# Attention pass of a four-layer graph network: where chunk sums, block steps and turned scores stand in VectorE's, ScalarE's and TensorE's order

## The chip, the cores and the metric

The kernel runs on one core of one Trainium2 chip. The metric is the device time of one execution in microseconds (us). Before the change it was 3532.23 us, the median of three runs (3505.18 to 3546.59).

## What is computed

A graph of 3125 nodes with 256 features and 53125 edges, sorted by their destination, goes through four graph layers, each with a residual and a layer norm. Only the first, an attention layer, is touched here:

```python
Q = (h @ Wq).reshape(n, H, HD); K = ...; V = ...            # 8 heads of 32
score = einsum('ehd,ehd->eh', Q[dst], K[src]) / sqrt(HD)
score = score + relu(efeat @ W1 + b1) @ W2 + b2             # a small MLP on 64 edge features
m = segment_max(score, dst); ex = exp(score - m[dst])
alpha = ex / segment_sum(ex, dst)[dst]
out = segment_sum(alpha * V[src], dst) @ Wo + bo
x = layernorm(x + out)
```

## The kernel before

The edges stand in tiles of 128; eight tiles are a *group* (1024 edges, 52 groups). Key and value rows of a group's sources are gathered into a ring of four buffers by indirect DMAs that GpSimd issues. A *chunk* is the group shifted by one tile; its value sums are added up one group behind the scores. A *block* is 128 destination nodes; every second group finishes one block, four pairs of groups behind.

The attention pass is one function `fused(g, k, i, b)` for each engine, run for group after group by `each_four` (L401): the first twelve groups are written out, then a loop takes four at a time, then two more. There is no planner: each engine runs its instructions in the order of its `fused`, and semaphores hold it back. A group with even k is called *even* here and one with odd k *odd*.

What one group g does, by the names in the code:

- TensorE: `turn_weights` (L1207) turns back the exponentials of chunk g-1. `q_rows` (L1183), once for each half, builds the query rows of four tiles in PSUM banks 0 and 1, which both halves share. `hidden` (L1155) is the MLP's first layer for group g+1. `tile_sums` (L1218) sums weighted value rows of chunk g-1, a half at a time. `turn_scores` (L1195) turns the scores of group g. `mlp_scores` (L1164) and `scores_back` (L1175) end the MLP for g+1. `window_sums` (L1234) puts the chunk's sums into their window of nodes. An even group ends with `turn_rows` (L1269) of a block, an odd one has `turn_back` (L1289) in its middle and `product` (L1296), the block's output projection, at its end.
- VectorE: `half_scores` (L1747), once for each half, multiplies query rows with gathered keys and reduces over a head (L1752, L1756). `weigh` (L1772, operations at L1780) multiplies value rows by their weights. `add_mlp` (L1759) finishes the scores of the group; `make_oht` and `make_narrow` build one-hots; `shift_scores` (L1794) runs two scans and a subtraction on the turned scores. `add_chunk` (L1808) adds the window sums to the accumulator, after a load of the window's first column from `chunk_i` into a register. For a block there are `rows_step` and `bias_step` (L1840, L1884), `norm_stats` (L1899) after the projection, and `norm_apply` (L1917) after ScalarE's two square roots.
- ScalarE: `weights_copy`, four `relu` (L840) on the MLP's hidden layer, `roots` (L912), `finish_rows` (L920), `stage_block` (L881), `turn_block` (L900), `sums_copy` (L862), `mlp_copy` (L842), and `exponent` (L848).

In VectorE's order before, a group ends with `shift_scores(g)`, then `add_chunk(g-1)`, then `rows_step` and `bias_step` (even) or `norm_stats` (odd). `add_chunk` waits for the window sums, `norm_stats` for the product. Then comes `half_scores(g+1, 0)`, which waits for `q_rows(g+1, 0)`.

Of the kernel before, what the change touches and what calls it, by code (L numbers as in the profile page):

```python
# [22 lines left out]
NG = -(-E // EG)  # L23
# [7 lines left out]
LAG = 3  # L31
# [8 lines left out]
CHUNKS = NG + 1  # L40
# [14 lines left out]
PASS_NONE, PASS_VALUE, PASS_GCN1, PASS_GCN2, PASS_SAGE, PASS_SG1, PASS_SG2, PASS_SG3 = range(8)  # L55
# [11 lines left out]
def gnn_program(nc, a, out):  # L67
    ctx = ExitStack()
    with ctx:
# [722 lines left out]
        def _(act):  # L792
# [40 lines left out]
            def windows_path():  # L833
                def relu(g, u):

                    c, half = u // 2, u % 2
                    act.wait_ge(hid_done, g * 4 + (u + 1))

                    wait(act, mlp_done, g)
                    nc.scalar.activation(hid[:, u, :], banks[:, 2 + half, :], ACT.Relu, bias=b1c[:, c:c + 1]).then_inc(hid_evac, 1)  # L840
# [13 lines left out]
                def weights_copy(c, k):  # L854
                    act.wait_ge(ex_back, c + 1)

                    wait(act, val_done, c * 2 - 2)
                    nc.scalar.activation(xcol[:, k, :, HEADS + 1:XW], ew_pad[:, bass.ds(c * TG, TG)].unsqueeze(2), ACT.Copy)
                    nc.scalar.activation(xcol[:, k, :, 0:HEADS], banks[:, S_BANK, EX_AT:EX_END].rearrange("p (t h) -> p t h", h=HEADS), ACT.Copy
                                         ).then_inc(ex_copied, 1)  # L860
# [39 lines left out]
                def turn_block(q, b):  # L900
                    if q in DENSE:
                        bank_sem = pe_a if q == PASS_SAGE else pe_b
                        before = blocks_before(q) + 1 if q == PASS_SAGE else blocks_before(q, TURNED)
                        act.wait_ge(bank_sem, b + (before + 1))
                        nc.scalar.activation(turned[:, :, :], banks[:, B_TURN, 0:D].rearrange("p (c n) -> p c n", c=FC), ACT.Copy  # L905
                                             ).then_inc(turn_done, 1)
# [53 lines left out]
                def fused(g, k, i, b):  # L960
                    full = not isinstance(g, int) or g < NG
                    blocks = not isinstance(b, int) or b >= 0
                    c, kc = g - 1, (k + 1) % 2
                    if not isinstance(g, int) or g:
                        weights_copy(c, kc)
                    if not isinstance(b, int) or b > 0:
                        if k % 2 == 0:
                            roots(PASS_VALUE, b - 1)
                    if full:
                        relu(g + 1, 0)  # L970
                        relu(g + 1, 1)
                    if blocks and k % 2 == 1:
                        turn_block(PASS_VALUE, b)
                    if not isinstance(b, int) or b > 0:
                        if k % 2 == 0:
                            finish_rows(PASS_VALUE, b - 1)
                    if full:
                        relu(g + 1, 2)
                        relu(g + 1, 3)
                    if blocks and k % 2 == 0:  # L980
                        stage_block(PASS_VALUE, b)
                    if not isinstance(g, int) or g:
                        sums_copy(c)
                    if full:
                        mlp_copy(g + 1, kc)
                    if not isinstance(g, int) or g < CHUNKS:
                        exponent(g)
# [81 lines left out]
        def _(pe):  # L1069
# [84 lines left out]
            def windows_path():  # L1154
# [28 lines left out]
                def q_rows(g, half):  # L1183

                    if half == 0:
                        pe.wait_ge(oht_ready, g + 1)
                    pe.wait_ge(qwin_done[half], g * 32 + 32)
                    wait(pe, qk_read, g * 2 + half)
                    for m in range(2):
                        for r in range(2):  # L1190
                            last = nc.tensor.matmul(banks[:, r, m * D:(m + 1) * D], oht[r * QW:(r + 1) * QW, half, m * P:(m + 1) * P],  # L1191
                                                    q_win[r * QW:(r + 1) * QW, half, :], start=True, stop=True)
                    last.then_inc(q_done, 1)
# [130 lines left out]
                def fused(g, k, i, b):  # L1324
                    full = not isinstance(g, int) or g < NG
                    value = not isinstance(g, int) or g > 0
                    blocks = not isinstance(b, int) or b >= 0
                    kc, kn = (k - 1) % RING, (k + 1) % 2
                    loads = (g + 1) // 2 + 1 if isinstance(g, int) else i * 2 + ((k + 1) // 2 + 1)
                    if value:  # L1330
                        turn_weights(g - 1)
                    if full:
                        q_rows(g, 0)
                        hidden(g + 1, kn, loads, 0)
                        q_rows(g, 1)
                    if blocks and k % 2 == 1:
                        wait(pe, chunk_added, g - 1)
                        turn_back(PASS_VALUE, b)
                    if full:
                        hidden(g + 1, kn, loads, 1)  # L1340
                    if value:
                        if blocks and k % 2 == 1:
                            pe.wait_ge(rows_done, b + 1)
                            pe.wait_ge(turn_done, b + 1)
                        elif blocks:
                            wait(pe, var_done, b)
                        tile_sums(g - 1, kc, 0)
                        tile_sums(g - 1, kc, 1)
                    if not isinstance(g, int) or g < CHUNKS:
                        turn_scores(g, k, i)  # L1350
                    if full:
                        mlp_scores(g + 1)
                        scores_back(g + 1, kn)
                    if value:
                        window_sums(g - 1, kc)
                    if blocks and k % 2 == 0:
                        turn_rows(PASS_VALUE, b)
                    if blocks and k % 2 == 1:
                        product(PASS_VALUE, b)
# [76 lines left out]
        def _(dve):  # L1436
# [24 lines left out]
            chain = Chain(link_sem)  # L1461
# [263 lines left out]
            def windows_path():  # L1725
# [237 lines left out]
                chain_at, size = chain_total(chain), LINKS[PASS_VALUE]  # L1963

                def fused(g, k, i, b):
                    static = isinstance(g, int)
                    full, value = not static or g < NG, not static or g > 0
                    blocks = not isinstance(b, int) or b >= 0
                    c, kc = g - 1, (k - 1) % RING
                    before = not static or b > 0  # L1970
                    if blocks and k % 2 == 0:
                        chain.enter(b * size + (chain_at - 4) if before else chain_at)
                    if full:
                        half_scores(g, k, i, 0)
                    if before and k % 2 == 0:
                        norm_apply(PASS_VALUE, b - 1)
                    if value:
                        weigh(c, kc, 0)
                    if full:
                        half_scores(g, k, i, 1)  # L1980
                    if value:
                        weigh(c, kc, 1)
                    if full:
                        add_mlp(g, k)
                        if k == RING - 1:
                            wrap_scores(i)
                        make_oht(g + 1)
                    if not static or g < CHUNKS:
                        make_narrow(g, k % 2)
                        shift_scores(g, k % 2, (g // 2 + 1) * (16 * TG) if static else i * (RING // 2 * 16 * TG) + (k // 2 + 1) * (16 * TG))  # L1990
                    if value:
                        add_chunk(c)
                    if blocks and k % 2 == 0:
                        rows_step(PASS_VALUE, b)
                        bias_step(PASS_VALUE, b)
                    if blocks and k % 2 == 1:
                        norm_stats(PASS_VALUE, b)
                        assert chain.leave() == (size if before else size - 4)

                each_four(dve, fused)  # L2000
                chain.enter(chain_at + (NG // 2 - LAG) * size - 4)
                norm_apply(PASS_VALUE, NG // 2 - LAG - 1)
                for b in range(NG // 2 - LAG, NB):
                    rows_step(PASS_VALUE, b)
# [3 lines left out]
                for q in GROUPED:  # L2008
# [44 lines left out]
                    size = LINKS[q]  # L2053
# [115 lines left out]
```

## Time and profile before

| | before |
|---|---|
| median of 3 runs | 3532.23 us |
| profiled execution | 3527.64 us |
| its span | 3525.7 us |
| TensorE busy | 2560.2 us (73%) |
| VectorE busy | 1970.7 us (56%) |
| GpSimd busy | 1737.9 us (49%) |
| ScalarE busy | 682.7 us (19%) |

The span is the time from the first to the last instruction of the profiled execution. The attention pass lies between about 126 us, where VectorE's first score product starts, and 1060 us; three gather passes and three dense passes follow. Busy shares are averages over all of these, so they say little of the attention pass: its own windows and its own chain of waits have to be read.

### The profile page before, as it was taken

How to read it: one execution, taken by the hardware profiler on the slowest of the kernel's cores; microseconds unless marked ns; L12 is line 12 of the kernel's file. 1: busy time of each engine (PE TensorE's matmuls, PEld its weight loads, DVE VectorE, ACT ScalarE, POOL GpSimd, SP SyncE). 2: the span in 40 equal slices, each digit the busy share in tenths (PEclk: the TensorE clock that was granted, in tenths of full speed). 3: DMA queues.
4: the chain of work that ended last, by engine and by line, in shares of the span. 5: the costliest groups of instructions: out<-in, count | busy, mean ns of one | idle time of the engine just before them, and what ended most of it. 6: DMA issues, size and time to landing. Idle time of an engine off the chain costs nothing.

```text
span 3525.7 us, 64349 instructions
## 1 busy us (share of the span) xinstructions
PE 2560.2 (73%) x18318; PEld 1985.6 (56%) x18422; DVE 1970.7 (56%) x6179; ACT 682.7 (19%) x1571; POOL 1737.9 (49%) x1779
## 2 busy tenths in 40 slices
PE   7566767666765565556767676577777699999997
PEld 6344334434435555554555555456665478888775
DVE  3477777676756555556667676667767621111222
ACT  3223333333330000001111111011111231111110
POOL 0554444444407777776777776677777500000000
PEclk9788887787766878787889888798889889999998
DMA  5876555565503333333333343333333322332221
GB/s 187 246 208 175 173 173 170 164 179 166 170 20 101 109 110 111 109 110 95 114 120 115 117 123 97 91 116 115 118 112 113 97 79 98 103 102 93 88 96 58
DMA packets 185480, 435.80 MB, mean 124 GB/s; under 512 B 42835, under 2 KB 89161, under 8 KB 185417
## 3 DMA queue, kind: packets, MB, share of 16 engines
q0 software_dynamic: 93184, 272.74, 26.7%
q1 hardware_dynamic: 88634, 159.04, 13.9%
q10 hardware_dynamic: 3600, 3.28, 0.3%
q8 instruction: 29, 0.48, 0.1%
q14 instruction: 33, 0.27, 0.0%
HBM read 390.37 MB, written 44.51 MB: 123 GB/s over the span
## 4 chain that ended last, share of the span: by engine, by line
PE 31%; POOL 26%; issue 21%; DVE 13%; DMA 6%; ACT 2%; SPq 1%; DVEq 1%; POOLq 0%; ACTq 0%
POOL gath L767 25%; PE banks L1411 15%; DVE prod L1752 3%; PE banks L1256 3%; DMA gath<-h_table,idx_slot 3%; PE banks L1239 2%; PE banks L1170 2%; DVE rh L1756 2%; DVE gath L1780 2%; DVE rh L1780 2%; PE banks L1303 1%; PE banks L1227 1%; DMA misc<-counts 1%; PE banks L1080 1%; PE banks L1242 1%
## 5 line engine op out<-in xcount | busy, mean ns | idle before, releaser
L767 POOL DMA_INDIRECT gath<-h_table,idx_slot x1248 | 1293.2, 1036 | 371.3 <-issue 344.5
L1256 PE MATMUL banks<-onehot,gath 128*128 128x128 f32 x4992 | 782.6, 323 | 479.8 <-DMA gath<-h_table,idx_slot 451.6
L1256 PEld LDWEIGHTS banks<-onehot,gath 128*128 128x128 f32 x4992 | 730.8, 233 | 538.0 <-DMA gath<-h_table,idx_slot 452.2
L1411 PE MATMUL banks<-gath,misc 128*128 128x256 bf16 x1875 | 516.5, 275 | 0.0
L1411 PE MATMUL banks<-acc,misc 128*128 128x256 bf16 x2500 | 421.4, 277 | 23.4 <-DMA misc<-counts 14.5
L765 POOL DMA_INDIRECT rh<-kv_table,idx_slot x208 | 211.1, 1015 | 215.3 <-PE banks L1230 163.1
L765 POOL DMA_INDIRECT gath<-kv_table,idx_slot x208 | 209.0, 1005 | 214.0 <-PE banks L1230 159.7
L1314 PE MATMUL banks<-gath 128*128 128x512 bf16 x624 | 243.7, 414 | 64.7 <-DVE gath L1958 64.7
L1411 PEld LDWEIGHTS banks<-acc,misc 128*128 128x128 bf16 x2500 | 243.4, 99 | 70.3 <-issue 16.8
L1958 DVE TENSOR_SCALAR gath<-w_qkv 128x800 bf16<-128x800 f16 x728 | 257.5, 424 | 0.0
L1838 DVE TENSOR_TENSOR acc<-acc,banks 128x256 f32 x156 | 65.3, 418 | 339.0 <-PE banks L1256 327.2
L1734 DVE TENSOR_SCALAR onehot<-iota_f,rel,ew_pad 128x128 f32<-128x128 f32 x832 | 224.8, 360 | 33.4 <-DVE x_rows L1934 18.9
L949 ACT ACTIVATE misc<-banks 128x512 f32 x104 | 62.1, 597 | 866.1 <-PE banks L1315 866.1
L1315 PE MATMUL banks<-gath 128*128 128x288 bf16 x728 | 223.6, 307 | 8.4 <-issue 3.7
L1411 PE MATMUL banks<-rh,misc 128*128 128x256 bf16 x1250 | 204.7, 273 | 0.0
L1411 PEld LDWEIGHTS banks<-gath,misc 128*128 128x128 bf16 x1875 | 185.4, 99 | 23.1
L1878 DVE SCALAR_TENSOR_TENSOR x_rows<-banks,node,x_rows 128x256 f32 (+1 forms) x50 | 24.2, 484 | 308.5 <-ACTq L1056 308.5
L1314 PEld LDWEIGHTS banks<-gath 128*128 128x128 bf16 x728 | 77.1, 106 | 164.6 <-DVE gath L1958 74.0
L1955 DVE TENSOR_SCALAR gath<-iota_f,src_lo 128x128 bf16<-128x128 f32 x728 | 156.0, 302 | 0.0
L1191 PE MATMUL banks<-q_win,rh 64*128 64x256 f32 x832 | 121.9, 403 | 46.9 <-DVE prod L1752 46.9
L840 ACT ACTIVATE onehot<-banks,b1c 128x512 f32<-128x512 f32 x212 | 133.6, 681 | 108.4 <-PE banks L1161 94.5
L1303 PE MATMUL banks<-w_lin,turned 128*128 128x256 f32 x400 | 124.9, 439 | 25.9 <-ACT turned L905 24.6
(217 smaller groups left out, 3552.4 us busy)
## 6 DMA issues: line engine op xcount, KB each, us to landing
misc<-counts SPq DMA_DIRECT2D x75, 800.0 KB, 4.3
counts<-misc SPq DMA_DIRECT2D x26, 800.0 KB, 3.9
gath<-h_table,idx_slot POOLq DMA_INDIRECT x1248
rh<-in_dst_rows SPq DMA_DIRECT2D x106, 128.0 KB
w_qkv<-in_ef_t SPq DMA_DIRECT2D x106, 128.0 KB
q_win<-q_table SPq DMA_DIRECT2D x208, 64.0 KB
rh<-mask_dram SPq DMA_DIRECT2D x424, 8.0 KB
kv_table<-onehot SPq DMA_DIRECT2D x25, 256.0 KB, 2.0
```

The source lines that it names most:

```text
L765: pool.indirect_dma_start(ring[m][:, t, :], None, source, row_index).then_inc(ring_in[m][t // HALF], 16)
L767: pool.indirect_dma_start(row_slot[:, k, t, :], None, source, row_index).then_inc(gath_done[k][t // HALF], 16)
L840: nc.scalar.activation(hid[:, u, :], banks[:, 2 + half, :], ACT.Relu, bias=b1c[:, c:c + 1]).then_inc(hid_evac, 1)
L1256: last = nc.tensor.matmul(banks[:, 3 * k + c, 0:P], row_slot[:, k, t, c * P:(c + 1) * P], onehot[:, k, t, :], start=(t == 0), stop=(t == T ...
L1303: last = nc.tensor.matmul(banks[:, B_ROWS, 0:D], turned[:, c, :], w_lin[:, DENSE[q], c, :], start=(c == 0), stop=(c == FC - 1))
L1314: nc.tensor.matmul(banks[:, 2, :], oh_src[:, t, :], oh_key[:, t, 0:512], start=(t == 0), stop=(t == ST - 1))
L1315: last = nc.tensor.matmul(banks[:, 5, 0:SC - 512], oh_src[:, t, :], oh_key[:, t, 512:SC], start=(t == 0), stop=(t == ST - 1))
L1411: last = nc.tensor.matmul(banks[:, slot, 0:D], c_slot[:, slot, c, :], parts[n % 2][j][:, c, :], start=(c == 0 and j == 0), stop=(c == NB - ...
L1734: last = nc.vector.tensor_scalar(onehot[:, k, t, :], iota_f[:, :], r, w[:, bass.ds(g * TG + t, 1)], ALU.is_equal, ALU.mult)
L1780: last = V.tensor_tensor(v, v, e.unsqueeze(3).to_broadcast([P, n, HEADS, HD]), ALU.mult)
L1955: V.tensor_scalar(oh_src[:, t, :], iota_f[:, :], src_lo[:, bass.ds(tile0 + t, 1)], None, ALU.is_equal)
L1958: last = V.tensor_scalar(oh_key[:, t, :], key_iota, key_tile[:, k, t:t + 1], None, ALU.is_equal)
```

## The change

No operation is added, removed or resized. In the attention pass three engines get another order:

- VectorE: the group's first half of scores comes first. Behind it stand `add_chunk` of chunk g-2 (it was chunk g-1 at the end of the group before), then `norm_stats(b-1)` in an even group, or `rows_step(b)` and `bias_step(b)` in an odd group. `norm_apply(b-1)` goes from before the first `weigh` to before the second.
- TensorE: `turn_scores` goes between the two halves of `tile_sums`; in an odd group the second `hidden` goes ahead of `turn_back`.
- ScalarE: `roots` goes behind the first two `relu`, `finish_rows` behind the last two.

```diff
@@ ScalarE
                     if not isinstance(g, int) or g:
                         weights_copy(c, kc)
+                    if full:
+                        relu(g + 1, 0)
+                        relu(g + 1, 1)
                     if not isinstance(b, int) or b > 0:
                         if k % 2 == 0:
                             roots(PASS_VALUE, b - 1)
-                    if full:
-                        relu(g + 1, 0)
-                        relu(g + 1, 1)
                     if blocks and k % 2 == 1:
                         turn_block(PASS_VALUE, b)
+                    if full:
+                        relu(g + 1, 2)
+                        relu(g + 1, 3)
                     if not isinstance(b, int) or b > 0:
                         if k % 2 == 0:
                             finish_rows(PASS_VALUE, b - 1)
-                    if full:
-                        relu(g + 1, 2)
-                        relu(g + 1, 3)
@@ TensorE
+                    if full:
+                        hidden(g + 1, kn, loads, 1)
                     if blocks and k % 2 == 1:
                         wait(pe, chunk_added, g - 1)
                         turn_back(PASS_VALUE, b)
-                    if full:
-                        hidden(g + 1, kn, loads, 1)
...
                         tile_sums(g - 1, kc, 0)
-                        tile_sums(g - 1, kc, 1)
                     if not isinstance(g, int) or g < CHUNKS:
                         turn_scores(g, k, i)
+                    if value:
+                        tile_sums(g - 1, kc, 1)
@@ VectorE
                     if full:
                         half_scores(g, k, i, 0)
+                    if not static or g > 1:
+                        add_chunk(g - 2)
                     if before and k % 2 == 0:
-                        norm_apply(PASS_VALUE, b - 1)
+                        norm_stats(PASS_VALUE, b - 1)
+                    if blocks and k % 2 == 1:
+                        rows_step(PASS_VALUE, b)
+                        bias_step(PASS_VALUE, b)
...
                     if value:
                         weigh(c, kc, 0)
                     if full:
                         half_scores(g, k, i, 1)
+                    if before and k % 2 == 0:
+                        norm_apply(PASS_VALUE, b - 1)
                     if value:
                         weigh(c, kc, 1)
...
-                    if value:
-                        add_chunk(c)
-                    if blocks and k % 2 == 0:
-                        rows_step(PASS_VALUE, b)
-                        bias_step(PASS_VALUE, b)
-                    if blocks and k % 2 == 1:
-                        norm_stats(PASS_VALUE, b)
...
                 each_four(dve, fused)
+                add_chunk(CHUNKS - 1)
...
+                norm_stats(PASS_VALUE, NG // 2 - LAG - 1)
                 norm_apply(PASS_VALUE, NG // 2 - LAG - 1)
```

Line numbers of VectorE's part are one higher in the changed kernel (L1753 for L1752 and so on).

**VectorE, from the end of an odd group into an even one.** `misc` and `acc` are `add_chunk`'s two sums, `ysum`, `stats` and `mv` are `norm_stats`, `prod` is the product of `half_scores`. Before:

```order
L1806 TENSOR_TENSOR rh<-banks,rh 64x128
L1809 TENSOR_LOAD chunk_i
L1809 ISA x2
L1814 ISA
L1814 TENSOR_TENSOR misc<-misc,banks 10x128
L1816 REGISTER_ALU
L1816 TENSOR_TENSOR acc<-acc,banks 128x2x128
L1912 TENSOR_TENSOR ysum<-banks,pre_b 128x256
L1913 BN_STATS stats<-ysum 128x6
L1915 BN_AGGR mv<-stats 128x2
L1752 TENSOR_TENSOR prod<-banks,rh 128x1024
```

With the change:

```order
L1807 TENSOR_TENSOR rh<-banks,rh 64x128
L1753 TENSOR_TENSOR prod<-banks,rh 128x1024
L1757 TENSOR_REDUCE rh<-prod 128x32
L1810 TENSOR_LOAD chunk_i
L1810 ISA x2
L1815 ISA
L1815 TENSOR_TENSOR misc<-misc,banks 10x128
L1817 REGISTER_ALU
L1817 TENSOR_TENSOR acc<-acc,banks 128x2x128
L1913 TENSOR_TENSOR ysum<-banks,pre_b 128x256
L1914 BN_STATS stats<-ysum 128x6
L1916 BN_AGGR mv<-stats 128x2
```

The chunk's sums and `norm_stats` stood between the last scan step and the next group's first product, and now stand behind that product and its reduction.

**VectorE, from the chunk's sum in an even group (before) or an odd one (now) to the next operation of the scores.** `blk_sc`, `node` and `rows` are `rows_step`, `pre_b` is `bias_step`. Before:

```order
L1816 TENSOR_TENSOR acc<-acc,banks 128x2x128
L1858 COPY blk_sc<-banks 128x10
L1859 TENSOR_SCALAR blk_sc<-blk_sc 128x1
L1860 TENSOR_SCALAR blk_sc<-blk_sc 128x1
L1861 TENSOR_SCALAR blk_sc<-blk_sc 128x8
L1862 TENSOR_SCALAR blk_sc<-blk_sc 128x1
L1863 TENSOR_SCALAR blk_sc<-blk_sc 128x1
L1864 RECIPROCAL node<-blk_sc 128x1
L1865 RECIPROCAL blk_sc<-blk_sc 128x8
L1866 TENSOR_TENSOR rows<-banks,blk_sc 128x256
L1888 TENSOR_TENSOR pre_b<-x_rows,bias 128x256
L1752 TENSOR_TENSOR prod<-banks,rh 128x1024
```

With the change:

```order
L1817 TENSOR_TENSOR acc<-acc,banks 128x2x128
L1859 COPY blk_sc<-banks 128x10
L1860 TENSOR_SCALAR blk_sc<-blk_sc 128x1
L1861 TENSOR_SCALAR blk_sc<-blk_sc 128x1
L1862 TENSOR_SCALAR blk_sc<-blk_sc 128x8
L1863 TENSOR_SCALAR blk_sc<-blk_sc 128x1
L1864 TENSOR_SCALAR blk_sc<-blk_sc 128x1
L1865 RECIPROCAL node<-blk_sc 128x1
L1866 RECIPROCAL blk_sc<-blk_sc 128x8
L1867 TENSOR_TENSOR rows<-banks,blk_sc 128x256
L1889 TENSOR_TENSOR pre_b<-x_rows,bias 128x256
L1781 TENSOR_TENSOR rh<-rh,xcol 128x256
```

The eleven operations were followed by the next group's first product (L1752); now they are followed by the first `weigh` (L1781) of a group whose first product is already done.

**TensorE, in the middle of an odd group.** L1161 is `hidden`, L1293 `turn_back`, L1227 and L1230 `tile_sums`, L1204 `turn_scores`, L1170 `mlp_scores`.

```order
 L1161 MATMUL banks<-w_qkv,w 128x512 x2
 L1191 MATMUL banks<-q_win,rh 128x256 x4
+L1161 MATMUL banks<-w_qkv,w 128x512 x2
 L1293 MATMUL banks<-ident,rows 128x128 x2
-L1161 MATMUL banks<-w_qkv,w 128x512 x2
 L1227 MATMUL banks<-gath,rh 32x256
 L1227 MATMUL banks<-rh 32x256 x3
 L1230 MATMUL banks<-xcol,rh 32x10 x4
+L1204 MATMUL banks<-ident,rh 64x128 x3
 L1227 MATMUL banks<-rh 32x256 x4
 L1230 MATMUL banks<-xcol,rh 32x10 x4
-L1204 MATMUL banks<-ident,rh 64x128 x3
```

The three turns of the scores now stand ahead of the second half of `tile_sums`, and `turn_back` behind the second `hidden`; an even group has the first of these two moves.

## Rows read from the trace of the kernel before

**Rows 1.** Windows, the pass's 38 groups from 307.56 us on; the columns stand first.
```profile
core 0: us, PE busy (x) PEld busy (x) DVE busy (x) ACT busy (x) POOL busy (x), PEclk, DMA share, GB/s
307.56:977.75 670.19, 464.27 (x3593) 270.06 (x3591) 478.11 (x1073) 241.71 (x533) 301.86 (x317) 0.80 0.58 169
```

**Rows 2.** Chain of waits from 551.09 to 622.77 us, shares by line.
```profile
by line: issue 17.0%; DVE prod L1752 13.3%; PE banks L1239 8.4%; DVE rh L1756 7.1%; DVE gath L1780 6.0%; DVE rh L1780 6.0%; PE banks L1227 5.4%; PE banks L1170 5.3%; PE banks L1242 4.2%; PE banks L1179 3.9%; PE banks L1303 3.6%; ACT w_qkv L
```

**Rows 3.** Timeline of VectorE, an even group: start, duration, engine, line, operation, idle before.
```profile
551.09 1.22 DVE L1752 TENSOR_TENSOR prod<-banks,rh 128x1024 f32<-128x1024 f32 x1
...
553.49 0.15 DVE L1930 RECIPROCAL blk_sc<-dstd 128x1 f32<-128x1 f32 x1
...
555.27 1.28 DVE L1780 TENSOR_TENSOR gath<-gath,xcol 128x256 f32<-128x256 f32 x2
556.47 1.22 DVE L1752 TENSOR_TENSOR prod<-banks,rh 128x1024 f32<-128x1024 f32 x1
...
558.86 1.22 DVE L1780 TENSOR_TENSOR gath<-gath,xcol 128x1024 f32<-128x1024 f32 x1
559.99 0.22 DVE L1765 SCALAR_TENSOR_TENSOR rh<-rh,banks 128x64 f32<-128x64 f32 x1
...
563.48 0.28 DVE L1806 TENSOR_TENSOR rh<-banks,rh 64x128 f32<-64x128 f32 x1
568.01 0.28 DVE L1814 TENSOR_TENSOR misc<-misc,banks 10x128 f32 x1 [4.25 <-PE banks L1242]
...
568.62 0.17 DVE L1858 COPY blk_sc<-banks 128x10 f32<-128x10 f32 x1
...
570.37 1.23 DVE L1752 TENSOR_TENSOR prod<-banks,rh 128x1024 f32<-128x1024 f32 x1
```

**Rows 4.** Timeline of VectorE, the end of the odd group that follows.
```profile
586.11 0.42 DVE L1912 TENSOR_TENSOR ysum<-banks,pre_b 128x256 f32<-128x256 f32 x1 [0.76 <-PE banks L1303]
...
587.15 0.18 DVE L1915 BATCH_NORM_AGGREGATE mv<-stats 128x2 f32<-128x6 f32 x1 [0.15 <-DVE stats L1913]
587.82 1.23 DVE L1752 TENSOR_TENSOR prod<-banks,gath 128x1024 f32<-128x1024 f32 x1 [0.49 <-issue]
```

**Rows 5.** Timeline of TensorE in the same two groups.
```profile
549.79 1.19 PE L1191 MATMUL banks<-q_win,rh 64*128 64x256 f32 x8
...
560.13 1.08 PE L1227 MATMUL banks<-gath,rh 128*32 128x256 f32 x8 [2.79 <-DVE gath L1780]
...
568.52 1.19 PE L1191 MATMUL banks<-q_win,rh 64*128 64x256 f32 x8
...
586.02 1.19 PE L1191 MATMUL banks<-q_win,rh 64*128 64x256 f32 x8
```

**Rows 6.** Timeline of TensorE and VectorE, start of a group that has no block yet.
```profile
209.70 1.28 PE L1191 MATMUL banks<-q_win,rh 64*128 64x256 f32 x8
...
211.09 1.23 DVE L1752 TENSOR_TENSOR prod<-banks,rh 128x1024 f32<-128x1024 f32 x1 [0.58 <-issue]
```

**Rows 7.** Waits of VectorE's 104 score products (L1752) on query rows: total us, times.
```profile
  PE banks L1191: 13.6, 2
```

**Rows 8.** Sequencer's own work: the register load of `add_chunk`, between 561 and 565 us.
```profile
L1809 DVEq TENSOR_LOAD <-chunk_i x1: 303/303/303, 563.6 to 563.6; - x1
```

**Rows 9.** Timeline of ScalarE: the exponentials of the group in rows 3.
```profile
565.77 0.31 ACT L852 ACTIVATE rh<-rh 64x128 f32<-64x128 f32 x1
```

**Rows 10.** Windows from the second `tile_sums` to the window sums, four groups.
```profile
218.34:222.93 4.59, 3.99 (x51) 2.58 (x52) 2.75 (x9) 1.46 (x4) 3.67 (x5) 1.00 0.64 172
560.13:567.87 7.74, 7.15 (x50) 4.10 (x50) 2.84 (x9) 2.74 (x5) 6.04 (x8) 0.50 0.80 234
577.62:584.60 6.98, 6.38 (x50) 3.81 (x50) 3.17 (x10) 1.34 (x4) 5.45 (x6) 0.57 0.78 226
596.99:603.78 6.79, 6.20 (x50) 3.58 (x50) 2.84 (x9) 2.74 (x5) 5.41 (x7) 0.60 0.74 217
```

**Rows 11.** Timeline of TensorE: `tile_sums` after a longer gap, near the pass's end.
```profile
1017.78 1.08 PE L1227 MATMUL banks<-rh 128*32 128x256 f32 x8 [4.83 <-DVE rh L1780]
```

More of the change, by code:

```diff
@@ L1971, in fused @@
                     if blocks and k % 2 == 0:
-                        chain.enter(b * size + (chain_at - 4) if before else chain_at)
+                        chain.enter(b * size + (chain_at + 4 - size) if before else chain_at)
                     if full:
                         half_scores(g, k, i, 0)
+                    if not static or g > 1:
+                        add_chunk(g - 2)
                     if before and k % 2 == 0:
-                        norm_apply(PASS_VALUE, b - 1)
+                        norm_stats(PASS_VALUE, b - 1)
+                    if blocks and k % 2 == 1:
+                        rows_step(PASS_VALUE, b)
+                        bias_step(PASS_VALUE, b)
+                        assert chain.leave() == (size if before else 4)
                     if value:
@@ L1990, in fused @@
                         shift_scores(g, k % 2, (g // 2 + 1) * (16 * TG) if static else i * (RING // 2 * 16 * TG) + (k // 2 + 1) * (16 * TG))
-                    if value:
-                        add_chunk(c)
-                    if blocks and k % 2 == 0:
-                        rows_step(PASS_VALUE, b)
-                        bias_step(PASS_VALUE, b)
-                    if blocks and k % 2 == 1:
-                        norm_stats(PASS_VALUE, b)
-                        assert chain.leave() == (size if before else size - 4)
                 each_four(dve, fused)
-                chain.enter(chain_at + (NG // 2 - LAG) * size - 4)
+                add_chunk(CHUNKS - 1)
+                chain.enter(chain_at + (NG // 2 - LAG) * size + (4 - size))
+                norm_stats(PASS_VALUE, NG // 2 - LAG - 1)
                 norm_apply(PASS_VALUE, NG // 2 - LAG - 1)
```

## The prediction

> **What bounds the kernel now.** I read the windows of the attention pass first, then the chain of waits in two pairs of groups, then the timelines of VectorE and TensorE side by side. The windows show a pass in which nobody is full: 38 groups take 670.19 us, 17.64 us each, with TensorE busy for 464.27 us of it, VectorE for 478.11 us and the transfers at 0.58 [rows 1]. So the groups are bound by a chain, not by an engine. The chain names VectorE's score products and `weigh` (L1752, L1756, L1780) and TensorE's matmuls (L1227, L1170, L1239, L1242) in turn, with no gather and hardly any ScalarE [rows 2]. The timelines show why: the two engines play ping-pong. From 551.09 to 560.08 us VectorE works without a pause (first half, `norm_apply`, first `weigh`, second half, second `weigh`) and TensorE waits [rows 3]; TensorE resumes at 560.13, after 2.79 us of idleness, and runs the rest of its group until the window sums end at 567.87 [rows 5, 10]. In this time VectorE finishes its one-hots and scans at 563.76 and idles 4.25 us [rows 3]. The reader is to see that this idle time is not what the group waits for: the next score product needs `q_rows`, which TensorE starts only at 568.52 [rows 5], in its own order behind the window sums. VectorE's work between the first score product and the second `weigh` stands on the chain with every nanosecond; its work between the scans and the window sums costs nothing; its work behind the window sums is partly covered by `q_rows`.
>
> **The change, part by part.** All times are from the profiled execution, 3527.6 us, which is 4.6 us below the median.
>
> *The new end of a group.* VectorE now goes from its scans straight to the next score product and is released by `q_rows`. In a group without a block this is so already: `q_rows` ends at 209.70 + 1.28 = 210.98 and the product starts at 211.09, 0.11 us later [rows 6]. Even group: `q_rows` ends at 568.52 + 1.19 = 569.71, so the product could start at 569.82 and starts at 570.37 [rows 3, 5]; saved 0.55 us. Odd group: 586.02 + 1.19 + 0.11 = 587.32 against 587.82, saved 0.50 us, where the loop turns [rows 4, 5]; in the other odd group 549.79 + 1.19 + 0.11 = 551.09, exactly where the product starts, nothing saved [rows 3, 5]. Mean for odd groups 0.25 us.
>
> *The new middle.* Behind the first half now stand, in every group, `add_chunk` (568.62 - 568.01 = 0.61 us), in odd groups `rows_step` and `bias_step` (570.37 - 568.62 = 1.75 us) [rows 3], in even groups `norm_stats` (587.15 + 0.18 - 586.11 = 1.22 us) [rows 4]. Could they be hidden there? Only by a wait for the second `q_rows` or for ScalarE's weights, and there is none: the product, its reduction, `norm_apply`, `weigh` and the second product follow one another without idle time [rows 3], and all 104 score products waited for `q_rows` only twice, 13.6 us [rows 7]. So they are added whole. `norm_apply` (555.27 - 553.49 = 1.78 us) only moves within the same stretch: nothing, in any order.
>
> *`add_chunk`'s register load* took 0.303 us on VectorE's sequencer, hidden in a wait. Bounds now: nothing, or 0.3 us in each of 50 groups, 15 us. I take nothing, since in the trace it ran from 563.6 us while the subtraction of 563.48 to 563.76 was still at work [rows 3, 8]; the 1.2 us reduction is a longer cover. No gain, since nothing is taken away.
>
> *`turn_scores` ahead of the second `tile_sums`.* It needs `add_mlp`, which ends at 559.99 + 0.22 = 560.21, where `tile_sums` needed only the second `weigh`, 560.08 [rows 3]. So TensorE's last stretch starts 0.13 us later, and the second `tile_sums`, all MLP work and the window sums are queued behind it. In return the scans start earlier, which is worth nothing: the exponentials ended at 566.08, 2.4 us before `q_rows` [rows 5, 9], and ScalarE runs them behind `mlp_copy`, not behind the scans.
>
> *ScalarE and TensorE's `turn_back`.* The roots now wait for `norm_stats`, about 4.2 us into the group, and are used by `norm_apply` at 7.8 us, where they were used at 2.4 before. `turn_back` waits for `rows_step` at about 4.4 us, and the first `tile_sums` waits for `weigh` until 6.0 us anyway. `finish_rows` and `stage_block` come out some 6 us later and are needed by `turn_rows` 18 us into the group. Nothing for all of these; if the cover went, `tile_sums` would be late by the difference.
>
> *The clock.* TensorE's idle stretch before its last matmuls grows. In an even group it lies between the first `weigh` and `add_mlp`'s end: second half 2.39, `norm_apply` 1.78 (it stood ahead of the first `weigh` before), second `weigh` 1.13, `add_mlp` 0.22, together 5.52 us [rows 3], less at most 1.08 for the first `tile_sums` [rows 5]: 4.4 us or more in place of 2.79. After a gap of 4.83 us the same eight matmuls took 1.08 us [rows 11], as they did at the 1.2 GHz level at 560.13 [rows 5, 10]. The stretch up to the window sums takes 7.74 us at a granted clock of 0.50, 6.79 us at 0.60, 4.59 us at 1.00 [rows 10]. Even groups shown have 7.74 and 6.79, mean 7.27; I put all of them at 7.74, 0.47 us more each. Bounds: nothing, or 7.74 in odd groups too (6.98 now), 0.76 us each. Odd groups stay as they are, since their gap grows by `add_mlp` alone, 0.22 us.
>
> The sum. Even groups 10 to 50 (21): 0.61 + 1.22 + 0.13 - 0.55 = 1.41 us, 29.6 us. Odd groups 9 to 51 (22): 0.61 + 1.75 + 0.13 - 0.25 = 2.24 us, 49.3 us. Groups 2 to 7 (6): 0.61 + 0.13, 4.4 us; group 8: 0.2 us. Together 83.5 us, and 21 times 0.47 for the clock, 9.9 us: 93 us. The two last groups and the other passes stay. 3527.6 + 93 = **3621 us**.
>
> **The rivals.** *The clock stays low in every group.* TensorE ran its last stretch at 0.50 to 0.60 of full speed in three of the four windows shown [rows 10]; if the longer gaps bring every odd stretch to 7.74 us as well, that is 22 x 0.76 = 17 us more, 3638 us. For it: the 4.83 us gap row. Against: odd gaps hardly grow. Chance 0.20. The Trainium skill, "TensorE: Matmul & The Clock Gate", Part 1, says that the throttled level is the default and that activity releases it; by that rule longer idle gaps speak for this rival, and the trace agrees as far as [rows 11] goes.
>
> *The clock rises: not slower.* The one place from which a gain can come is the same stretch. It takes 4.59 us at 1.00 against a mean of (7.74 + 6.98 + 6.79) / 3 = 7.17 us, 2.58 us a group. If the new rhythm kept the clock at 2.4 GHz in all 44 groups, that would be 113 us back: 3527.6 + 83.5 - 113 = 3498 us. It decides from 83.5 / 2.58 = 32 of 44 groups on; below that the kernel is slower. For it: the stretch at 218.34, in a group without block work. Against it: that group came after less idle time, and the change adds to it. Chance 0.08.
>
> *The moved work is covered after all.* If the second score product had to wait for `q_rows(g, 1)`, or `weigh` for the weights, the additions would vanish and the savings remain: 22 x (0.55 + 0.25) = 18 us, 3510 us, no change that can be told. Against it stands the uninterrupted timeline and the two waits in 104. Chance 0.08.
>
> The forecast keeps 0.64.
>
> **How the numbers follow.** The forecast's own range: from 83.5 us less 5.5 us (odd groups save 0.50 us each) and no clock, 78 us, to 93 us plus 5.5 (odd groups save nothing) plus 15 (the register load), 114 us: 3606 to 3642 us. The clock rival reaches 3638 + 20.5 = 3659. The runs of before lie 27 us below and 14 above their median, so I widen by about 20 us downward and 10 upward: 3585 to 3670 holds forecast and clock rival, and leaves out the other two, 0.16. One per cent, about what a measurement of this kernel can tell from no change, is 35 us, 3497 to 3567. Covered work (0.08) falls inside it; the rising clock lies at its lower edge, half inside and half below (0.04 each); of the other cases I leave 0.01 for a change half as large. So faster 0.04, same 0.13, slower 0.83.
>
> **What would show it.** The attention pass takes some 40 us for two groups where it took 35.3. VectorE's first product is released by `q_rows` (L1191) in nearly every group, 0.1 us after its end; from there to the second `weigh`'s end it works without a pause, 10.8 us in even groups and 9.5 in odd ones, against 9.0 and 7.2. TensorE's wait for `add_mlp` (L1765) takes the place of the wait for `weigh`, 4.4 us or more in even groups. VectorE's wait for the window sums (L1242) is gone and one of about the same length stands in front of L1753. ScalarE's exponentials still end well before `q_rows`. The prediction is wrong if VectorE pauses between its two halves, or if the pass's granted clock rises well above 0.80 [rows 1].

## The result, and the profile after

The changed kernel takes 3576.4 us (median of four runs, 3569.55 to 3584.52) against 3539.31 us for the kernel before, re-timed beside it: ratio 1.0117, 95% interval 1.0078 to 1.0155. It is slower by 1.2%, as forecast in sign, by 37 us where 93 were forecast, and below the range's lower end of 3585.

The profiled execution after has a span of 3567.7 us, 42.0 more. The attention pass alone is longer by more: the first half of group 50 starts at 1029.70 us in place of 977.75, 52 us later, and the first gather of the pass behind it (L767) starts at 1113.6 us in place of 1061.1. What follows, whose code is unchanged, takes some 10 us less in this pair of executions; in the thirteen profiles of this case the time from the first half of group 50 to the end lies anywhere between 2516 and 2552 us. So the part that the prediction was about grew by some 52 us in the profile, and 93 were forecast for it.

The 38 groups 12 to 49 after, in the columns of [rows 1]:

```profile
316.34:1029.70 713.36, 436.24 (x3593) 250.29 (x3591) 471.22 (x1073) 244.44 (x532) 301.91 (x317) 0.78 0.54 159
```

Two groups take 713.36 / 19 = 37.55 us, before 35.27 [rows 1]. TensorE runs the same 3593 matmuls but is busy for 436.24 us in place of 464.27, although the mean granted clock is lower, 0.78 against 0.80. Both facts together are the key to the miss.

VectorE in an odd and an even group after, the counterpart of [rows 3, 4]:

```profile
560.97 1.23 DVE L1753 TENSOR_TENSOR prod<-banks,gath 128x1024 f32<-128x1024 f32 x1 [5.84 <-PE banks L1191]
...
563.37 0.27 DVE L1815 TENSOR_TENSOR misc<-misc,banks 10x128 f32 x1
...
563.89 0.15 DVE L1859 COPY blk_sc<-banks 128x10 f32<-128x10 f32 x1
...
570.35 0.21 DVE L1766 SCALAR_TENSOR_TENSOR rh<-rh,banks 128x64 f32<-128x64 f32 x1
...
579.15 1.23 DVE L1753 TENSOR_TENSOR prod<-banks,rh 128x1024 f32<-128x1024 f32 x1 [5.84 <-PE banks L1191]
...
589.67 0.21 DVE L1766 SCALAR_TENSOR_TENSOR rh<-rh,banks 128x64 f32<-128x64 f32 x1
```

The idle time in front of the window sums (4.25 us) is gone, and 5.84 us of idle time stand in front of the score product, released by `q_rows` (L1191). Between the product and `add_mlp` VectorE never pauses for more than 0.15 us: 9.38 us in the odd group and 10.52 in the even one. The count over the whole pass, first of L1753 and then of the chunk's sum (L1815):

```profile
  PE banks L1191: 292.7, 52
```

```profile
  PE banks L1242: 11.4, 3
```

Before, the product waited for `q_rows` twice, 13.6 us [rows 7]; now it does in every group. The chunk's sum waited for the window sums all 53 times before, 183.2 us; three waits are left. TensorE in the odd group after:

```profile
570.71 0.82 PE L1204 MATMUL banks<-ident,rh 128*64 128x128 f32 x3 [2.91 <-DVE rh L1766]
...
572.44 1.91 PE L1170 MATMUL banks<-onehot,rh 128*32 128x256 f32 x16
...
575.26 1.06 PE L1239 MATMUL banks<-rh 128*128 128x128 f32 x8
...
577.86 1.18 PE L1191 MATMUL banks<-q_win,rh 64*128 64x256 f32 x8
```

`turn_scores` (L1204) now waits for `add_mlp` (L1766), and `q_rows` ends at 579.04, 0.11 us before the product, as in [rows 6]. The MLP scores (L1170) still run at the 1.2 GHz level, 1.91 us at a granted clock of 0.50, but the window sums (L1239) take 1.06 at 1.00. In the odd group of [rows 4] before they took 1.92, at 0.50:

```profile
581.74 1.92 PE L1239 MATMUL banks<-rh 128*128 128x128 f32 x8
```

### The profile page after: what moved, and what is told of

It is laid out like the page before. It is cut to its first block, busy times and chain, and to the rows that moved or that the text cites. A ratio compares the mean times of both kernels' runs of the same rounds, so it can differ in the third digit from the quotient of the medians.

```text
span 3567.7 us, 64359 instructions
## 1 busy us (share of the span) xinstructions
PE 2522.5 (71%) x18318; PEld 1957.9 (55%) x18422; DVE 1962.7 (55%) x6179; ACT 685.4 (19%) x1571; POOL 1729.0 (48%) x1779
## 3 DMA queue, kind: packets, MB, share of 16 engines
q10 hardware_dynamic: 3600, 3.28, 0.3%
## 4 chain that ended last, share of the span: by engine, by line
PE 34%; POOL 25%; issue 20%; DVE 11%; DMA 5%; DVEq 2%; ACT 1%; SPq 1%; POOLq 0%; ACTq 0%
POOL gath L767 25%; PE banks L1412 16%; DVE prod L1753 3%; PE banks L1256 3%; DMA gath<-h_table,idx_slot 3%; PE banks L1170 3%; PE banks L1303 2%; PE banks L1239 2%; PE banks L1227 2%; PE banks L1191 1%; PE banks L1204 1%; PE banks L1080 1%; DVE rh L1757 1%; DVE rh L1781 1%; PE banks L1179 1%
## 5 line engine op out<-in xcount | busy, mean ns | idle before, releaser
L767 POOL DMA_INDIRECT gath<-h_table,idx_slot x1248 | 1282.1, 1027 | 371.4 <-issue 344.7
L1204 PE MATMUL banks<-ident,rh 128*64 128x128 f32 x159 | 42.5, 404 | 191.2 <-DVE rh L1766 191.2
L1753 DVE TENSOR_TENSOR prod<-banks,rh 128x1024 f32<-128x1024 f32 x52 | 63.4, 1220 | 148.7 <-PE banks L1191 148.7
```

Of the source, the lines that this page charges most:

```text
L767: pool.indirect_dma_start(row_slot[:, k, t, :], None, source, row_index).then_inc(gath_done[k][t // HALF], 16)
L1753: V.tensor_tensor(prod_half.rearrange("p (r m) d -> p r m d", r=2), banks[:, 0:2, :].rearrange("p r (m d) -> p r m d", m=2), ring[k][:, ha ...
```

## The experiments

Each ran in at least three rounds beside the kernel before; ratios are to that. Two theories were set against each other. **A (the clock):** the moved work costs what the sum says, and the shortfall is the clock term. **B (the order):** the clock has little to do with it, the new order of TensorE shortens the chain.

**e1 and e2: the clock held.** TensorE's idle stretches are filled with matmuls on a block of zeros whose results nobody reads; e1 is the kernel before, e2 the changed one. They write to the PSUM bank of the window sums, so they wait until VectorE has added these (`chunk_added`), as the first `tile_sums` does anyway. The comments are added here and give e2's counts.

```diff
+                        wait(pe, chunk_added, g - 1)
+                        keep_busy(4 if k % 2 else 20)      # e2: 6, 20
                         tile_sums(g - 1, kc, 0)
+                        keep_busy(32 if k % 2 else 32)     # e2: 34, 58
```

> The kernel before, with idle stretches of TensorE in the attention pass filled by matmuls whose results nobody reads (20 or 4 ahead of the first tile_sums, 32 behind it, each 128x128 bf16). Theory A (the clock): the forecast missed because the clock's cost in the stretch from the second weigh to the window sums was mis-sized, not because moved work was hidden. It expects a granted clock near 1.0 in the pass, that stretch near 4.6 us in place of about 7, and 2.4 us in some 44 groups, about 105 us less than the kernel before, some 3435 us. Theory B (the order): the clock has little to do with it and the new order of TensorE shortened that stretch; it expects at most 20 us less, as matmuls are in TensorE's way or not.

> The changed kernel with such matmuls in its idle stretches (20 or 6 ahead of the first tile_sums, 58 or 34 behind it). With the clock held in both kernels only the order differs. Theory A expects the changed kernel to be slower than e1 by what the moved work costs without the clock, 83.5 us by the prediction's sum and about 75 us by the durations in its own trace, twice the 37 us measured without filling: some 3515 us. Theory B expects the same difference as without filling, 30 to 45 us.

Measured: e1 3394.71 us, ratio 0.9652 [0.9624, 0.968]; e2 3465.26 us, ratio 0.9865 [0.9843, 0.9886]. The windows of the 38 groups, e1 and then e2:

```profile
289.73:870.80 581.07, 471.84 (x5265) 315.89 (x5263) 477.01 (x1073) 243.76 (x533) 300.74 (x318) 1.00 0.67 196
```

```profile
300.41:943.69 643.28, 511.30 (x5835) 361.69 (x5833) 471.38 (x1073) 245.72 (x532) 305.65 (x318) 0.97 0.61 177
```

The clock is held in e1 (1.00) and nearly so in e2 (0.97), and the difference between the two orders is 70.6 us, 3.28 us for two groups (30.58 and 33.86). In e2 the clock still fell in 11 of the 19 odd groups; they took 16.87 us in the mean and the other eight 16.45, so 4.6 of the 62.2 us between the two windows are the clock's, and pairs of groups without such a fall differ by 3.0 us. Without filling the difference is 37 us and 2.28. That is nearer to theory A's figures (75 to 83.5 us) than to B's (30 to 45): the order costs some 65 to 70 us, and in the unfilled pair the clock gives a part of it back. By the Trainium skill, "TensorE: Matmul & The Clock Gate", Part 1, activity releases the throttled level; that filling idle time with useless matmuls takes 119 us off agrees with it. From the second `tile_sums` to the end of the window sums, an odd and an even group of e1:

```profile
558.05:562.58 4.53, 3.93 (x50) 2.52 (x50) 2.75 (x9) 1.46 (x4) 3.60 (x4) 1.00 0.75 192
573.97:578.51 4.54, 3.94 (x50) 2.53 (x50) 2.77 (x9) 2.74 (x5) 3.62 (x5) 1.00 0.66 197
```

4.53 us in both, as the one undisturbed stretch of [rows 10] had it, 4.59.

**e3 and e4: the turn alone.** e3 is the kernel before with `turn_scores` between the two halves of `tile_sums`; e4 is the changed kernel with it behind both.

```diff
                         tile_sums(g - 1, kc, 0)
-                        tile_sums(g - 1, kc, 1)
                     if not isinstance(g, int) or g < CHUNKS:
                         turn_scores(g, k, i)
+                    if value:
+                        tile_sums(g - 1, kc, 1)
```

> The kernel before with one part of the change: turn_scores between the two halves of tile_sums. Theory A expects 0.13 us more in 50 groups, 6 us, which is no change that can be told. Theory B expects most of the shortening of the stretch, about 1 us in 44 groups: 40 us less than before, some 3500 us.

> The changed kernel with turn_scores behind both halves of tile_sums again, all else as changed. Theory A expects some 6 us less than the changed kernel, about 3570 us. Theory B expects the stretch to grow again by about 1 us in 44 groups: 40 us more, about 3617 us.

Measured: e3 3477.22 us, 0.9889 [0.9872, 0.9907], a gain of 36 us that theory A had not expected and theory B had (40); e4 3577.25 us, 1.0165 [1.0133, 1.0197], whose interval overlaps the changed kernel's: neither 6 us less nor 40 more, which leaves both theories where they were. In single traces e4 reaches group 50 14 us later than the changed kernel, 12 of them before group 12, and e3 26.5 us earlier than the kernel before: the gain of the turn's place does not carry over whole to the changed order. The 38 groups of e3:

```profile
305.82:951.25 645.43, 429.77 (x3593) 249.55 (x3591) 475.44 (x1074) 242.42 (x533) 303.17 (x318) 0.85 0.61 176
```

The same 3593 matmuls keep TensorE busy for 34.5 us less than before [rows 1], at a granted clock of 0.85 in place of 0.80. So e3's gain looked like the clock's too, and theory A was amended: a small edit to the order can move the low stretch. e5 and e6 test that.

**e5: the turn alone, clock held.** e1 with the edit of e3.

> e1 (the kernel before, idle stretches filled) with turn_scores between the two halves of tile_sums, the edit of e3. e3 took 36 us off, which theory A did not expect. If that gain is the clock's (it returned earlier in the stretch, theory A amended), it is gone where the clock is held: e5 is at e1's time plus 0.13 us in 50 groups, 6 us, ratio to before near 0.967. If the order itself saves time (theory B), e5 is again some 36 us below e1, ratio near 0.955.

Measured: 3398.02 us, 0.9673 [0.9639, 0.9706]. Where the clock cannot move, the turn ahead of the sums gains nothing (e1 0.9652; 30.65 us for two groups against 30.58). So theory B is out for this move: e3's gain came from the clock.

**e6: a longer gap without another order.** The kernel before, its second `tile_sums` waiting for `add_mlp`.

```diff
                         tile_sums(g - 1, kc, 0)
+                        if full:
+                            pe.wait_ge(s_ready, g + 1)
                         tile_sums(g - 1, kc, 1)
```

> The kernel before, in its own order, with one wait more: the second tile_sums waits for add_mlp as turn_scores does in e3, so that TensorE's gap is longer by the same 0.13 to 0.3 us and nothing else differs. Theory A amended (the length of the gap sets when the low clock begins and ends) expects a gain of 20 to 40 us, like e3's. Theory B expects 6 us more than before, ratio 1.002.

Measured: 3517.13 us, 1.0000 [0.9978, 1.0022]; the pass's clock is 0.80 and TensorE busy for 464.54 us, both as before. The gap is 3.00 us in even groups and 2.89 in odd ones, as long as e3's (3.01 and 2.90; before 2.76 and 2.69), and the 38 groups take 679.13 us, 8.9 more than before: the longer gap is paid and nothing comes back. The amendment's mechanism falls: a gap longer by that little does not by itself move the low stretch. What in e3 does, turned scores as the first matmuls after the gap or the shift against the groups' rhythm, stays open.

**e9: the chunk's sum alone, clock held.** e5 with only `add_chunk` moved between the halves (and two useless matmuls more in even groups; the last ends 1.06 us before `turn_scores` can start).

```diff
                     if full:
                         half_scores(g, k, i, 0)
+                    if not static or g > 1:
+                        add_chunk(g - 2)
...
-                    if value:
-                        add_chunk(c)
```

> e5 (turn_scores ahead, idle stretches filled) with add_chunk alone moved between the halves; block steps stay at the end of a group. If the moved work is on the chain whole, as the prediction's sum has it, this costs 0.52 to 0.61 us in some 44 groups with block work and in the early ones, 25 to 30 us on e5: some 3425 us, and the block steps account for the rest of the 70 us between e1 and e2. If the moved work were partly hidden between the halves, e9 is within 10 us of e5.

Measured: 3450.66 us, 0.9777 [0.973, 0.9824]. Two groups take 31.88 us, 1.23 more than in e5: 0.61 us a group, the duration that the sum took from [rows 3]. That agreement is in part luck: the clock fell in five of e9's 38 groups, which cost 0.7 us each, and nearly all groups without such a fall take 0.52 us more than their counterparts in e5 (16.77 against 16.25, 14.74 against 14.22). That is the time from `add_chunk`'s start to the next operation in the trace after, 563.37 to 563.89. The block steps, with the smaller moves and the savings at the end of a group, make up the rest of the way to e2: 33.86 - 31.88 = 1.98 us for two groups, 1.92 where the clock did not fall; the sum had 1.22 + 1.75 - 0.55 - 0.25 = 2.17. By the ratios the two steps are 1.0 and 0.9 points; the first is 37 us and more than the 25 to 30 expected, but up to group 50 the traces of e9 and e5 differ by 31. So the chunk's sum is not hidden at all, and of the block steps little or nothing.

**e7, e8, e10, e11: the wait that the change uncovered.** If VectorE waits for `q_rows` alone, TensorE can run it earlier. e7 puts `q_rows(g + 1, 0)` ahead of the window sums, e10 ahead of the MLP scores, both in three of four groups; e10 also puts the window sums ahead of `scores_back`, in every group. e8 and e11 are e7 and e10 with filled idle stretches. e10:

```diff
                     if full:
-                        q_rows(g, 0)
+                        if k == 0:
+                            q_rows(g, 0)
                         hidden(g + 1, kn, loads, 0)
...
                     if full:
+                        if k < RING - 1 and (not isinstance(g, int) or g + 1 < NG):
+                            q_rows(g + 1, 0)
                         mlp_scores(g + 1)
-                        scores_back(g + 1, kn)
                     if value:
                         window_sums(g - 1, kc)
+                    if full:
+                        scores_back(g + 1, kn)
```

> The changed kernel with q_rows of the next group's first half ahead of the window sums instead of behind turn_weights, in three of four groups (not across the loop's turn). Both theories say that VectorE waits there for q_rows alone, so the window sums, turn_rows or product and turn_weights leave the chain: about 2.5 us in 38 groups, 95 us less than the changed kernel if the clock does not eat it, some 3480 us, below the kernel before. The clock can take up to half of it.

> e7 with the idle stretches filled as in e2. With the clock held the gain of hoisting is whole: e2's time less 2.2 us (window sums 1.53, turn_rows 0.55 or product 1.07, at the high clock) in 38 groups, 85 us: some 3380 us, ratio to before 0.962, at or below e1's 0.965. This is the version meant to beat both.

> The changed kernel with q_rows of the next group's first half ahead of the MLP scores, and the window sums ahead of scores_back, in three of four groups. The prediction's reading (the next score product waits for q_rows alone) expects VectorE to go from its scans into the next product without the wait of 5.8 us; add_chunk then waits about 1 us for the window sums. 3 to 5 us in 38 groups less than the changed kernel, 115 to 190 us: 3390 to 3460 us, more if the clock rises with it.

> e10 with the idle stretches filled (12 or 4 ahead of the first tile_sums, 44 or 28 behind it). With the clock held and the wait for q_rows gone, a pair of groups should take some 27 us in place of 33.9 (e2): 130 us less than e2 at most, with one group in four unchanged some 100 us: about 3365 us, below e1 and e8.

Measured: e7 3475.3 us, 0.9902 [0.9865, 0.9938]; e8 3397.91 us, 0.966 [0.9624, 0.9697]; e10 3425.5 us, 0.9701 [0.9659, 0.9742]; e11 3364.51 us, 0.9532 [0.9473, 0.959]. e7, e10 and e11 did what was expected; e8 gained 2.05 points on e2, 72 us where 85 were expected, and is level with e1, not below it. In e11 the score product waits for `q_rows` 25 times in place of 52:

```profile
  PE banks L1191: 61.0, 25
```

e11, the changed order of VectorE with earlier query rows and a held clock, is the fastest version run here, 4.7% below the kernel before; without useless matmuls e10 is 3.0% below it.

## Why the prediction was wrong, point by point

- *What bounds the kernel:* right. VectorE between the product and the second `weigh`, then TensorE to `q_rows`, whose only other wait there is a short one for ScalarE's `mlp_copy` (0.59 us before L1179); e10 and e11 gain by this reading.
- *The new end of a group:* right. The product is released by `q_rows` in every group, 0.11 us after its end in the group shown.
- *The new middle:* right in kind and nearly in size. Forecast 9.5 and 10.8 us to the second `weigh`'s end; measured to `add_mlp`'s start 9.38 and 10.52. With the clock held the chunk's sum costs 0.52 us a group where 0.61 were taken, and the block steps 1.9 to 2.0 us a pair where 2.17 were.
- *The register load* and *ScalarE, `turn_back`:* nothing, as taken. No wait of VectorE longer than 0.15 us appears between the halves. The first `tile_sums` of the odd group waits for ScalarE's copy behind `turn_back` and starts at 567.12, 0.2 us after `weigh`; it is off the chain, since TensorE then waits for `add_mlp` until 570.71.
- *`turn_scores` ahead:* 0.13 us was taken as its whole price. With the clock held it is no more than that (e5 against e1: 0.07 us for two groups, 0.26 were taken). Without, the same edit alone is worth 36 us by way of the clock (e3), which the prediction did not see as possible.
- *The clock:* **this step failed, in size and in sign.** The prediction put every even stretch at 7.74 us, the price of a clock low throughout, left the odd ones as they were, and added 9.9 us. The gaps grew as it said: to 4.89 us in the mean of the even groups, where 4.4 or more were forecast, and to 2.89 in the odd ones. The work behind them became shorter, not longer. The prediction priced when the clock falls, and left out that it then returns earlier in the work. Stretches after, `turn_scores` to the window sums' end, even, odd, even, odd:

```profile
552.54:559.17 6.63, 6.03 (x50) 3.45 (x50) 2.52 (x8) 2.74 (x5) 3.70 (x6) 0.59 0.84 243
570.71:576.80 6.09, 5.49 (x50) 2.91 (x50) 2.53 (x8) 1.34 (x4) 4.57 (x6) 0.64 0.77 223
590.03:596.66 6.63, 6.04 (x49) 3.44 (x50) 2.54 (x8) 2.74 (x5) 4.60 (x7) 0.58 0.80 241
608.23:614.32 6.09, 5.50 (x50) 2.90 (x50) 2.98 (x9) 1.34 (x4) 4.57 (x6) 0.64 0.73 224
```

All four are shorter than the three of [rows 10] outside the early groups, 7.74, 6.98 and 6.79. But those three were few to judge by: in the 38 groups before, the stretch takes anything from 5.86 to 7.74 us, and 7.27, which the sum took as the mean of the even groups, is their mean only in the two shown. The same windows added up over all 38 groups, before and then after:

```profile
sum 260.26, PE 237.66 PEld 139.02 DVE 110.81 ACT 77.78 POOL 197.04; mean PE 6.25 PEld 3.66 DVE 2.92 ACT 2.05 POOL 5.19
```

```profile
sum 243.35, PE 220.68 PEld 121.99 DVE 100.15 ACT 77.66 POOL 162.64; mean PE 5.81 PEld 3.21 DVE 2.64 ACT 2.04 POOL 4.28
```

Even groups went from 6.96 us to 6.60 in the mean, where 7.74 were forecast, and odd ones from 6.74 to 6.21, where no change was. Together that is 16.9 us less in the 38 groups, where the sum had 19 x 0.47 = 8.9 us more. Where the low clock went is seen in the idle stretch ahead of them, before (even, odd) and after (odd, even):

```profile
557.33:560.13 2.80, 0.01 (x2) 0.01 (x1) 2.77 (x5) 0.25 (x1) 1.64 (x2) 0.64 0.16 26
574.93:577.62 2.69, 0.00 (x2) 0.00 (x1) 2.66 (x4) 0.57 (x1) 1.53 (x2) 1.00 0.19 38
```

```profile
567.80:570.71 2.91, 0.00 (x1) 0.03 (x1) 2.88 (x5) 0.00 (x0) 1.75 (x2) 0.58 0.13 30
585.23:590.03 4.80, 0.01 (x2) 0.03 (x1) 4.15 (x12) 1.12 (x3) 3.33 (x3) 0.51 0.35 86
```

Before, the gap was granted 0.64 and 1.00; after, 0.58 and 0.51. In the mean of the 38 groups it was 0.68 (even) and 0.94 (odd) before and 0.53 and 0.56 after, while the stretches went from 0.59 and 0.61 to 0.60 and 0.65. The low clock now falls on idle time, where it costs nothing, and is over sooner once work resumes. That is why the pass can have a lower mean clock and 28 us less of busy TensorE, and why the prediction's own sign for a wrong clock term, a mean clock well above 0.80, did not show. What in the new order brings the clock back sooner is not isolated: e6 shows that a slightly longer gap alone does not, and e3 that the turn's place alone can.

The account of the 38 groups, in microseconds: forecast 69.4 for the order (19 pairs at 1.41 + 2.24) and 8.9 for the clock, together 78.3; measured 43.2 (713.36 - 670.19). The order alone is 62.2 by e2 less e1, 57.6 without the clock's part in e2: 7 to 12 less than forecast. The stretches gave back 16.9 where 8.9 were added: 26 less, the larger part of the miss. 57.6 - 16.9 is 40.7, so 2.5 of the 43.2 stay unexplained. Over the whole pass the growth is 52; from there to the measured 37 lie the unchanged passes, 10 us shorter in this pair of executions, and the spread of the runs.

- *The rivals.* Theory A's mechanism is the rival "the clock rises" at part of its size: some 17 us were given back in the 38 groups, where not being slower needed 83.5 in all. The chance went to a clock held in all groups, and the cases between were left out of the range. The rival of a clock low throughout, which the Trainium skill's rule was weighed for, did not come: its longer gap came, its longer work did not. Covered work is refuted by e9 for the chunk's sum, and for the block steps by what e2 costs beyond it.

## What to carry to other kernels

Filling one engine's idle time with work taken from behind a wait costs that work whole if the new place lies on the chain: ask what the idle engine is waiting for next (here `q_rows`, in TensorE's own order), and move that first, as e7 and e10 did. Where the granted clock switches within each period, price a change in the gaps from both sides, the fall and the return, and measure the order with the clock held: two filled kernels separated some 70 us of order from the 37 that the plain timing showed. Read the low stretches of every period, not of a few: here they took from 5.86 to 7.74 us in one kernel.

## What the runs showed of the hardware that was not expected

TensorE's useless matmuls took 119 us off the kernel (ratio 0.9652) by holding the granted clock at 1.00 in place of 0.80 in the 38 groups; some 105 were expected of it. A turn of scores that comes as the first work after the gap raised the pass's clock from 0.80 to 0.85 and saved 36 us (e3), while an equally long gap without the new order gave nothing back (e6).
